# Cross attention with negated scores, one signal per batch, masks made a group ahead and x normalised first

## The reference

```python
x = x + L0_xattn(layernorm(x), ctx)       # stage A, mLSTM cell with 8 heads
x = x + L0_ffn(layernorm(x))              # stage B, hidden 768
x = x + L1_xattn(layernorm(x), ctx, mask) # stage C
x = x + L1_ffn(layernorm(x))              # stage D, four layers, hidden 1024

def _L1_xattn_ref(x1, x2, x2_mask, W, diagonal):
    x1_rep = relu(einsum('bld,hd->blh', x1, W))
    x2_rep = relu(einsum('bld,hd->blh', x2, W))
    scores = einsum('bih,bjh->bij', x1_rep * diagonal, x2_rep)
    m = (1.0 - x2_mask) * -10000.0
    alpha = softmax(scores + m[:, None, :], axis=-1)
    return einsum('bij,bjd->bid', alpha, x2)
```

## Time and profile before

| what | us |
|---|---|
| median of 3 runs | 586.76 (586.48 to 586.87) |
| the profiled execution, its time | 586.5 |
| its span in the profile | 584.9 |
| PE busy | 548.8 (94%) |
| DVE busy | 330.9 (57%) |
| ACT busy | 230.3 (39%) |
| POOL busy | 80.1 (14%) |

### The profile page before, as it was taken

The page is one execution under the profiler, slowest core; times in us unless marked ns, Lnnn a source line. Parts: engine busy times, 40 slices in busy tenths (PEclk is TensorE's granted clock), DMA queues, the critical chain, the costliest instruction groups (busy, mean ns, idle before and its releaser), DMA issues.

```text
span 584.9 us, 8490 instructions
## 1 busy us (share of the span) xinstructions
PE 548.8 (94%) x2765; PEld 446.0 (76%) x2773; DVE 330.9 (57%) x802; ACT 230.3 (39%) x436; POOL 80.1 (14%) x121
## 2 busy tenths in 40 slices
PE   6698988999999998899999999999999999999993
PEld 5476665688888877678888878888788888788883
DVE  6569889778777588663353453443543534633331
ACT  2244645547788644362122251122441122621120
POOL 5223324202311233100000100000000001000001
PEclk9999999999999999999999999999999999999998
DMA  7675628344958797200000000000000000000001
GB/s 198 161 167 169 143 79 194 115 162 140 391 190 234 208 322 147 81 1 0 1 0 1 36 2 1 0 1 9 28 0 1 1 1 37 0 1 0 1 0 38
DMA packets 57760, 47.69 MB, mean 82 GB/s; under 512 B 37278, under 2 KB 48542, under 8 KB 57316
## 3 DMA queue, kind: packets, MB, share of 16 engines
q1 hardware_dynamic: 51960, 28.29, 18.7%
q0 software_dynamic: 5616, 18.88, 9.7%
q10 hardware_dynamic: 148, 0.04, 0.0%
HBM read 40.58 MB, written 2.10 MB: 73 GB/s over the span
## 4 chain that ended last, share of the span: by engine, by line
PE 67%; DVE 4%; ACT 2%; issue 1%; POOL 0%; DVEq 0%; ACTq 0%; POOLq 0%
PE ps L896 54%; PE ps L588 4%; PE ps L589 4%; PE ps L574 1%; DVE xn L1248 1%; PE ps L843 1%; PE ps L580 1%; PE ps L584 1%; PE ps L581 1%; ACT al L1175 1%; ACT h L1211 0%; DVE sc L1493 0%; DVE x L1518 0%; DVE x L1460 0%; ACT kr L1162 0%
## 5 line engine op out<-in xcount | busy, mean ns | idle before, releaser
L896 PE MATMUL ps<-hBt,h 128*128 128x512 f32 x512 | 117.9, 390 | 0.1
L896 PE MATMUL ps<-hA,h 128*128 128x512 f32 x512 | 117.3, 390 | 0.0
L1211 ACT ACTIVATE h<-ps,scol 128x512 f32<-128x512 f32 x64 | 44.2, 690 | 175.4 <-PE ps L896 175.3
L896 PEld LDWEIGHTS ps<-hBt,h 128*128 128x128 f32 x512 | 95.7, 188 | 20.8 <-DVE hBt L1539 1.1
L896 PEld LDWEIGHTS ps<-hA,h 128*128 128x128 f32 x512 | 95.9, 188 | 20.4 <-DVE hA L1539 0.6
L896 PE MATMUL ps<-xT,w 128*128 128x512 f32 x256 | 61.9, 396 | 1.8 <-DVE h L1534 1.1
L896 PEld LDWEIGHTS ps<-xT,w 128*128 128x128 f32 x256 | 46.2, 188 | 15.9 <-issue 6.6
L1557 DVE CAST hBt<-h 128x512 fp32r<-128x512 f32 x32 | 13.7, 427 | 73.7 <-ACT h L1211 73.7
L1557 DVE CAST hA<-h 128x512 fp32r<-128x512 f32 x32 | 13.7, 427 | 70.0 <-ACT h L1211 70.0
L431 POOL TENSOR_TENSOR rstd<-ve,mhalf 128x4 f32<-128x4 f32 x16 | 16.7, 1046 | 207.9 <-DVE ve L1243 207.9
L1194 ACT ACTIVATE silD<-ps,scol 128x512 f32<-128x512 f32 x32 | 22.0, 688 | 47.5 <-PE ps L896 47.5
(11 more groups left out here) (175 smaller groups left out, 895.8 us busy)
## 6 DMA issues: line engine op xcount, KB each, us to landing
looked<-w_all_in SPq DMA_DIRECT2D x16, 704.0 KB, 5.6
h<-w_all_in POOLq DMA_DIRECT2D x16, 512.0 KB, 6.5
V<-ctx_in SPq DMA_DIRECT2D x32, 128.0 KB, 4.4
Qb<-xT SPq DMA_DIRECT2D x64, 64.0 KB, 2.1
w<-w_all_in POOLq DMA_DIRECT2D x3, 1024.0 KB, 7.0
x<-x_in SPq DMA_DIRECT2D x4, 512.0 KB, 4.9
kstA<-ctxT_in SPq DMA_DIRECT2D x4, 512.0 KB, 5.4
kstC<-ctxT_in SPq DMA_DIRECT2D x4, 512.0 KB, 5.7
```

Of the source, the lines that this page charges most:

```text
L896: last = mm(o, a, b, start=(k == 0 and p == 0), stop=(k == n_k - 1 and p == 1))
L1211: fn(h32[:, m % 2, :], ps[:, 2 + m % 4, :], ACT.Gelu, scale=scol[:, L + 1, m:m + 1])\
```

## The change

In stage C the sign of the scores is turned: `diag` is negated once in stage A, the mask is built with the other sign, DVE takes the minimum, and ACT computes exp(-s + min), so that the separate negation goes. `sm_ready` counts batches instead of groups. The mask of the next group is made at the end of the current one. x_norm stands before scale_queries. The value adds become a function, which for the last group stands behind the first h32 of stage D. The statistics and normalisation of x number 9 move from the start of stage C into the last group of stage B. PE's wait for the last residual add at the start of C goes; the flag's sum and comparison move to the second group, its read to the end of stage C. The first tiles of stage D wait for each half of x_lo apart. On POOL and ACT the context's k_lo and k_hi move to the front of their group's step.

```diff
@@ POOL
             with pool.Fori(0, 2) as i:
                 for u in range(2):
                     g = 2 * i + u
+                    with pool.If(i < 1):
+                        k_lo(G + 2 + u, kstC[:, u, :, :], u)
                     for c in range(MD // G):
...
-                    with pool.If(i < 1):
-                        k_lo(G + 2 + u, kstC[:, u, :, :], u)
@@ PE
             def stage_c(loop):
-                pe.wait_ge(s["xB_done"], NB + 2)
                 pe.wait_ge(s["l0_lo"], KD)
-                pe.wait_ge(s["flag_sums"], 2)
-                mm(ps[0:1, OB, 0:1], fsum[:, 1:2], onec[:, :], start=True, stop=True).then_inc(s["flag_tot"], 1)
+                pe.wait_ge(s["silu_ready"], MB * G + 2)
                 keys(0, 0)
                 queries(0, 0)
-                pe.wait_ge(s["flag_ready"], 2)
-                flag_d = pe.value_load(fint[0:1, 1:2])
+
+                def flag_total():
+                    pe.wait_ge(s["flag_sums"], 2)
+                    pe.wait_ge(s["at_ready"], 2)
+                    mm(ps[0:1, ATB, 0:1], fsum[:, 1:2], onec[:, :], start=True, stop=True).then_inc(s["flag_tot"], 1)
...
+                        if u == 1:
+                            only_first(loop, i, flag_total)
                         scores(g)
                         if loop or g < G - 1:
                             more(lambda: keys(gn, 1 - u))
+                            if u == 1:
+                                pe.wait_ge(s["flag_ready"], 2)
                             turn_al(g)
...
-                return flag_d
+                return pe.value_load(fint[0:1, 1:2])
...
-            def first_tile(a, w, bank, m):
-                for k in range(KD):
+            def first_tile(w, bank, m, ks=range(KD)):
+                for k in ks:
+                    pe.wait_ge(s["xlo_done"], KD * 3 * G + k + 1)
                     last = wide(ps[:, bank + m, :], lambda k, p: w[:, k, m * P:(m + 1) * P],
                                 lambda k, p: xT[:, 0, p, k, :], k, KD, False)
...
-                pe.wait_ge(s["xlo_done"], KD * (3 * G + 1))
-                first_tile(0, w1, 2, 0)
-                first_tile(0, w1, 2, 1)
-                pe.wait_ge(s["sm_ready"], G + 1)
+                for k in range(KD):
+                    for m in range(2):
+                        first_tile(w1, 2, m, (k,))
+                pe.wait_ge(s["sm_ready"], Q * (G + 1))
@@ ACT
+                    if_more(act, i, lambda: k_hi(4, kstC[:, u, :, :], u))
                     x_hi(2 * G + g + 1, 1 - u)
-                    act.wait_ge(s["sm_ready"], g + 2)
                     for q in range(Q):
-                        fn(al[:, q, :], sc[:, q, :], ACT.Exp, bias=nmx[:, q:q + 1], accum_out=rsm[:, q:q + 1])\
-                            .then_inc(s["al_ready"], 1)
+                        act.wait_ge(s["sm_ready"], Q * g + Q + q + 1)
+                        fn(al[:, q, :], sc[:, q, :], ACT.Exp, bias=nsm[:, q:q + 1], scale=-1.0,
+                           accum_out=rsm[:, q:q + 1]).then_inc(s["al_ready"], 1)
                     more(lambda: relu_keys(gn))
-                    with act.If(i < 1):
-                        k_hi(4, kstC[:, u, :, :], u)
@@ DVE, stage A
+            v.tensor_scalar(diag[:, :], diag[:, :], -1.0, None, ALU.mult).then_inc(s["ndiag"], 1)
@@ DVE, end of stage B
                     if q == 2:
                         x_lo(G + g + 1, 1 - u)
+                        if g == G - 1:
+                            dve.wait_ge(s["xB_done"], 2 * Q + 2)
+                            x_stats(2 * G + 1, Q)
...
+                if g == G - 1:
+                    x_norm(2 * G + 1, Q)
             dve.wait_ge(s["xB_done"], NB + 2)
-            x_stats(2 * G + 1, Q)
-            x_norm(2 * G + 1, Q)
@@ DVE, stage C
+            def mask(g):
+                dve.wait_ge(s["mask_ld"], 16 * (g + 1))
+                v.tensor_scalar(mf[:, :, :], mk[:, :, :], NEG, -NEG, ALU.mult, ALU.add).then_inc(s["mask_free"], 1)
+            def add_values(g):
+                dve.wait_ge(s["rrs_ready"], g + 1)
+                for q in range(Q):
...
             scale_queries(0)
+            mask(0)
...
-                    dve.wait_ge(s["mask_ld"], 16 * (g + 1))
-                    v.tensor_scalar(mf[:, :, :], mk[:, :, :], -NEG, NEG, ALU.mult, ALU.add).then_inc(s["mask_free"], 1)
                     if u == 1:
+                        if_more(dve, i, flag_two)
                         if_later(dve, i, lambda: x_lo(3 * G, 0))
...
-                        ch.step(v.tensor_tensor_reduce(sc[:, q, :], ps[:, SCB, q * S:(q + 1) * S], mf[:, q, :], 1.0,
-                                                       -BIG, ALU.add, ALU.max, smx[:, q:q + 1]))
-                    ch.settle()
-                    v.tensor_scalar(nmx[:, :], smx[:, :], -1.0, None, ALU.mult).then_inc(s["sm_ready"], 1)
+                        v.tensor_tensor_reduce(sc[:, q, :], ps[:, SCB, q * S:(q + 1) * S], mf[:, q, :], 1.0, BIG,
+                                               ALU.add, ALU.min, nsm[:, q:q + 1]).then_inc(s["sm_ready"], 1)
                     more(lambda: x_lo(2 * G + g + 1, 1 - u))
...
-                    more(lambda: scale_queries(gn))
                     if u == 0:
                         x_norm(2 * G + g + 2, 8 - 8 * i)
                     else:
                         more(lambda: x_norm(2 * G + 3, 3 * Q))
...
+                    more(lambda: scale_queries(gn))
+                    more(lambda: mask(gn))
+                    v.reciprocal(rrs[:, :], rsm[:, :]).then_inc(s["rrs_ready"], 1)
+                    more(lambda: add_values(g))
@@ DVE, stage D
                             v.scalar_tensor_tensor(out=h32[:, m % 2, :], in0=ps[:, 4 + m % 2, :],
...
+                            if g == 0 and m == 0:
+                                add_values(G - 1)
```

More of the change, by code:

```diff
@@ L156, in two_layers @@
         den = place(base, "den", [P, 3, 2, Q], F32)
-        smx = place(base, "smx", [P, Q], F32)
-        nmx = place(base, "nmx", [P, Q], F32)
+        nsm = place(base, "nsm", [P, Q], F32)
         rsm = place(base, "rsm", [P, Q], F32)
@@ L1227, in _ @@
             dve.sem_inc(s["qrc_done"], KD)
-            dve.sem_inc(s["sm_ready"], 1)
+            dve.sem_inc(s["sm_ready"], Q)
             dve.sem_inc(s["at_ready"], 1)
@@ L1463, in _, with flag_two @@
                         head_norm(NB + q - Q, q)
+                if g == G - 1:
+                    x_norm(2 * G + 1, Q)
             dve.wait_ge(s["xB_done"], NB + 2)
-            x_stats(2 * G + 1, Q)
-            x_norm(2 * G + 1, Q)
+            dve.wait_ge(s["ndiag"], 1)
+            def mask(g):
[4 more added lines that the diff above has]
+                for q in range(Q):
+                    b = Q * g + q
+                    if q % 2 == 0:
+                        dve.wait_ge(s["av_done"], b + 2 * Q + 2)
+                    v.scalar_tensor_tensor(out=x[:, b, :], in0=ps[:, OB + q // 2, (q % 2) * D:(q % 2 + 1) * D],
+                                           scalar=rrs[:, q:q + 1],
+                                           in1=x[:, b, :], op0=ALU.mult, op1=ALU.add).then_inc(s["xC_done"], 1)
+            def flag_two():
+                dve.wait_ge(s["flag_tot"], 2)
+                v.tensor_scalar(fint[:, 1:2], ps[0:1, ATB, 0:1], 0.0, None, ALU.is_gt).then_inc(s["flag_ready"], 1)
             def scale_queries(g):
@@ L1474, in scale_queries @@
                         .then_inc(s["qrc_done"], 1)
-            dve.wait_ge(s["flag_tot"], 2)
-            v.tensor_scalar(fint[:, 1:2], ps[0:1, OB, 0:1], 0.0, None, ALU.is_gt).then_inc(s["flag_ready"], 1)
             scale_queries(0)
+            mask(0)
             with dve.Fori(0, 2) as i:
@@ L1510, in _ @@
                         more(lambda: x_norm(2 * G + 3, 3 * Q))
-                    ch.step(v.reciprocal(rrs[:, :], rsm[:, :]))
-                    ch.settle()
-                    ch.end()
-                    for q in range(Q):
-                        b = Q * g + q
-                        if q % 2 == 0:
-                            dve.wait_ge(s["av_done"], b + 2 * Q + 2)
-                        v.scalar_tensor_tensor(out=x[:, b, :], in0=ps[:, OB + q // 2, (q % 2) * D:(q % 2 + 1) * D],
-                                               scalar=rrs[:, q:q + 1],
-                                               in1=x[:, b, :], op0=ALU.mult, op1=ALU.add).then_inc(s["xC_done"], 1)
-            dve.wait_ge(s["av_done"], NB + 2 * Q)
-            dve.wait_ge(s["xC_done"], NB + 2)
+                    more(lambda: scale_queries(gn))
+                    more(lambda: mask(gn))
+                    v.reciprocal(rrs[:, :], rsm[:, :]).then_inc(s["rrs_ready"], 1)
+                    more(lambda: add_values(g))
             for i in range(2):
```

11 lines of the change are left out of this document (5 added, 6 removed).

## The result

| | us |
|---|---|
| before, median of 4 runs | 586.82 (586.48 to 587.71) |
| after, median of 4 runs | 579.75 (578.64 to 580.5) |
| ratio | 0.9875, 95% interval 0.9854 to 0.9896 |
| forecast | 581.3, range 580.0 to 583.9 |

The kernel became faster by 7.1 us, where 5.4 were forecast. It ended 0.25 us under the low end of the range.

The account below looks back on a forecast made before the run. TensorE, busy 94% of the span, bounds the kernel; its idle time around stage C can be won. 0.64 + 3.6 + 1.0 + 1.25 - 0.12 = 6.4 us, less 1.0 for collisions, gave 581.3 us, range 580.0 to 583.9.

Parts of the forecast that it names:

- uncollided sum: Stage C and its two ends: all gains added, before any charge for collisions or late transfers, 6.4 us.
- Handover: Stage B to C: PE no longer waits for the last add or makes the flag's matmuls there, 0.64 us.
- Two cycles: Stage C's group-to-group loop: cycle of 10.5 us in place of 12.3, 3.6 us for two; flag's matmuls cost 0.12.
- Third cycle: Last group of stage C up to stage D's first weight matmul, still waiting for x_lo: gain 1.0 us.
- Tail: Start of stage D: PE's pause for h32 falls away, less 0.15 waiting for h32(1); gain 1.25 us.
- What is pushed into what: Stage C: late mask loads and k_lo(7) or k_hi(7) in the way, charged 1.0 us together, between 0 and 3.
- No collision: Rival: k_lo(7) falls between x_norm(10) and x_norm(11), masks in time; gain 6.4 us, 580.3; chance 0.2.
- Both harms: Stage C: mask(g+1) stalls for its load, 0.5 to 1 us; k_lo(7) sits on mask(1), 0 to 1.6.
- The question left to be seen: Stage C: whether POOL's k_lo can stop DVE's mask; by the port rule mask(1) can lose up to 2.35 us.
- Transfers late: Rival: kstC lands at 214.9 as before, delaying stage C's exponentials 2.2 us; gain 3.7, 583.0; chance 0.17.
- VectorE the bound: Rival: conditional blocks and waits make DVE's stage C ring 11.2 us instead of 10.5; gain 4.3, 582.5; chance 0.12.
- Slower: Rival: k_hi(7) stands before x_hi and exp on ACT; kstC landing at 218.6 uses up the gain; chance 0.03.

Follow-up runs that it names:

- xlo_tail: Changed kernel with the third group's value adds behind the last score pass and w2's first tile behind the weights' transposes; 577.19 us, ratio 0.9834.
- u_tail: Changed kernel with the last group's value adds again before stage D's first h32; 579.83 us, ratio 0.9895.
- u_klo: Changed kernel with POOL's k_lo again behind the power for the next x_norm; 581.97 us, ratio 0.9929.
- early_kst: Changed kernel with the second kstC load issued by SP right behind the first; 582.66 us, one run.
- u_handover: Changed kernel with PE waiting again for the last residual add, and statistics and normalisation of x number 9 back at stage C's start; 581.32 us, ratio 0.9932.
- kst_late: Changed kernel with the second kstC load held back some 10 us, until group 0's value adds are done; 585.01 us, one run.
- u_mask: Changed kernel with the mask made again at the start of its own group; 580.58 us, ratio 0.9899.
- w_later: Changed kernel with the three weight loads issued by POOL inside the loop, behind the power of x_norm(11); 589.35 us, ratio 1.0036.

## Why the prediction came out as it did

**The uncollided sum held.** It was 6.4 us; the ladder gives 6.68.
- *Handover*: 0.64 forecast, 0.92 measured. PE's idle of 0.52 and the flag's 0.12 were right, but a matmul that follows unbroken starts before the one ahead has ended. The keys now start 0.12 after stage B's last matmul instead of 0.92, and the first of them takes 0.23 until the next in place of 0.34. The prediction used this overlap in the tail and forgot it here.
- *Two cycles*: 3.6 less the flag's 0.12, that is 3.48, forecast; 3.50 measured. The steps are in their places: exponentials at T+0.33 to 0.43 (T+0.4), x_norm T+5.34 (5.45), scalings T+6.66 (6.75), cycle 10.43 (10.5). The flag's two matmuls cost what was set down or less; with the first cycle at 10.59 and the second at 10.43, 0.16 at most is theirs.
- *Third cycle*: 1.0 forecast, 1.08 measured. PE's 0.96 for x_lo is the wait named there, and xlo_tail removed it.
- *Tail*: 1.25 forecast, 1.18 measured. u_tail puts 0.89 of it on the adds. The other 0.3 was not separated from x_lo's wait per half. The 0.15 for h32(1) is there: around the start of the fourth tile two matmuls start 0.37 apart (243.93 and 244.30) in place of 0.23. But not the adds delay h32(1), which were over at 242.48; it waits 0.92 for ScalarE:

```profile
243.40 0.75 DVE L1551 SCALAR_TENSOR_TENSOR h<-ps,scol,silD 128x512 f32<-128x512 f32 x1 [0.92 <-ACT silD L1198]
```

- The value load at the end of C shows no cost beside the wait for x_lo, nor in xlo_tail, where that wait is gone. Its cost is near 0 with or without the cover.

**The step that failed is the charge under "What is pushed into what"**: 1.0 us for collisions and late transfers, measured 0. Without it the forecast is the rival *No collision*, 580.3, and that is what happened. Of the 1.7 us by which the median gained more than forecast, 1.0 is this charge and 0.3 the sum (nearly all of it the handover); the other 0.4 is not in the stretch from M to X, and no edit was found to account for it. The range ended 0.3 under the collision-free case, with no room for a sum 0.3 too small or for the spread of the kernel itself (578.64 to 580.5).

Two sizes in the charge were off. The V loads took 2.77 us to issue and not 5.78, which the prediction had taken over from before. From 211 to 216 us the DMA engines moved 140 GB/s against 313 in before. The cause is the place of POOL's h2 loads. In before they left 0.5 us ahead of the V loads of 212.96:

```profile
212.45 1.29 POOL L535 DMA_DIRECT2D h<-w_all_in  x2
```

In after they stand behind k_lo(7) and left at 215.86, 5 us behind V's start at 210.82. The prediction wrote that they now leave behind k_lo(7) and didn't draw this from it. All profiles agree. Where the h2 loads left ahead of V or with it, the issue took 5.78 (before), 5.97 (u_klo) and 6.04 (early_kst); in the eleven where they left 3.0 us or more behind V's start, 2.76 to 3.78. u_klo changes nothing but k_lo's place, and h2's with it. That the weights leave sooner is not the cause: in u_klo and early_kst they left at M+1.70 as in after. So mask(2) was issued at 213.83 and not 217, and had 8 us until its use. And kstC landed at 212.35, just past the late end of the estimate of 210 to 212: late enough for k_lo(7) to miss mask(1) by 1.9 us, early enough for the exponentials to lose only 0.1.

**Both harms are real; the kernel sits between them.** This is shown from both sides. With k_hi(7) at T-1.48 (after) the exponentials start 0.1 later and the cycle loses nothing (10.43, and 10.44 in early_kst, where k_hi(7) is long done); at T-0.10 (u_handover) it loses 1.3, at T+4.24 (kst_late) 8. Earlier (early_kst) costs 1.84. A mask in k_lo's way (u_mask) costs 2.0. Each harm has an edge: on one side of it nothing is lost, beyond it about the overlap. In u_handover the exponentials start 1.38 later and the cycle is 1.32 longer. A mask that begins 0.22 after k_lo loses 2.03 (u_mask), one that begins 1.77 after it 0.48 (mask(0) in after). The prediction was right to see two tight places and wrong to charge an average of them, since the kernel lies on the free side of both.

**The question left to be seen**, whether k_lo can stop the mask, has an answer: 2.45 us in place of 0.42. The Trainium skill's page "SBUF — State Buffer", section "Who interferes with whom", says that a VectorE instruction in a two-port mode, which a tensor_scalar can be, and a GpSimd instruction shut each other out, and that the one that comes first keeps the ports to its end. u_mask, u_klo and early_kst agree: the first x_norm instruction takes 2.44 in u_klo, and x_norm 3.42 in early_kst. So does w_later, where the mask came first. In the kernel after, k_lo(7) runs beside the score pass (0.28 to 0.29 an instruction) and x_lo (1.28 for two), and k_lo(6) beside a scaling of the queries (0.75); these read PSUM and keep their lengths.

**The rivals.** *Transfers late* didn't come in the kernel after, though u_handover shows 1.3 us of it. *VectorE the bound* is refuted: cycles of 10.43 and 10.59, not 11.2. *Slower* has its mechanism confirmed by kst_late, but its price was too low. The break-even worked out, 218.6, is M+23.85 of before; kst_late's kstC landed at M+23.8, and its ladder is already 1.3 us above that of before. The missing term is the clock, some 2 us once PE has stood for 4.30. By its device time this one run stayed under before's median all the same (585.01 and 586.77).

**The parts don't add up.** The six undone edits cost 11.1 us together, the whole change 6.68. Each undo leaves the others in a schedule that they no longer fit: u_klo hurts because x_norm stands first, u_mask because k_lo stands first and so runs at the start of a group. The change is one schedule, and an undo prices its fit in that schedule and not its share of the gain.

## What to carry to other kernels

When an edit moves work on one engine, look for the earliest and the latest time at which each neighbour can stand it, and price both edges: a load that lands sooner can hurt as much as one that lands late. Do not charge the mean of a harm that has an edge; forecast the side on which the times put it, and give the other side its own size, from the overlap, and its own chance. When a queue's transfers change places with another's, do not take over how long they took to issue. Put GpSimd's tensor work where VectorE has instructions that read PSUM.

## What the runs showed of the hardware

- The granted clock falls to 0.50 after PE stood 4.30 us (kst_late) and 7.67 us (w_later), and twelve matmuls then take 5.1 us in place of 2.8 to 3.0. In the kernel after, where PE's longest wait between M and D is 0.96 us, every window of 5 us from 196 to 216 shows 1.00.
- Four V loads take SP from 2.77 us (after) through 3.78 (kst_late) and 5.78 to 11.86 (w_later) to issue. Two h2 loads of 512 KB that leave with them or just ahead (before, u_klo, early_kst) double the time; three weight loads of 1 MB and two of h2 just ahead make it 11.86, where the same group has 4.53 in after. A mask load behind them inherits all of it. The same kstC load took from 4.4 (kst_late) to 11.7 us.
- A VectorE tensor_scalar on SBUF that begins while GpSimd's 128x1024 tensor_tensor runs ends 0.15 to 0.3 us after it (u_klo, u_mask, mask(0) in after). One that began 0.07 before it kept its 0.42 (w_later).
- Nearly the same code in stages A and B gets a different clock from execution to execution, and the whole span moves with it. Windows of 30 us, first one of before and then one of after:

```profile
0.00:30.00 30.00, 20.92 (x82) 15.00 (x84) 17.97 (x51) 7.78 (x13) 11.34 (x20) 0.96 0.69 179
```

```profile
90.00:120.00 30.00, 26.84 (x147) 19.19 (x146) 23.89 (x73) 15.99 (x41) 7.95 (x17) 0.94 0.45 127
```

The other profiles have such windows elsewhere or not at all, all of them before 120 us: u_tail has 0.94 from 60 to 90, u_handover and u_klo have none. M follows their number: without a dip M is 192.69 and 193.23, with one window under 1.00 it is 193.21 to 194.72, with two 194.75 to 196.55, with three 196.81 and 198.13 (fourteen profiles, four windows each). What sets the dip off was not found.
